# Block-diagonal column transforms of a Fourier mixing stage, issued as tiles of 64 rows

## The reference, cut to what matters

```python
xn = _layernorm(x, norm1_w, norm1_b)
xf = jnp.fft.rfft2(xn, axes=(1, 2), norm='ortho')          # (8, 32, 17, 192), complex
xf = xf.reshape(B, h, w // 2 + 1, NB, BS)                   # 8 channel blocks of 24
o1 = jnp.einsum('bhwni,hwnio->bhwno', xf, w1c) + b1c        # its own 24x24 matrix per (h, w, block)
o1 = jax.lax.complex(jax.nn.relu(o1.real), jax.nn.relu(o1.imag))
xs = jnp.fft.irfft2(o1.reshape(B, h, w // 2 + 1, C), s=(h, w), axes=(1, 2), norm='ortho')
xm = _layernorm(xs, norm2_w, norm2_b)
hdn = jax.nn.gelu(xm @ mlp_w1 + mlp_b1, approximate=False)
return xs + x + hdn @ mlp_w2 + mlp_b2
```

## Time and profile before

| | us |
|---|---|
| median of 3 runs (1192.73 to 1200.53) | 1198.21 |
| the profiled execution, its own time | 1196.19 |
| its span, first to last instruction | 1194.4 |
| mean granted clock of TensorE, as a share of full speed | 0.956 |
| TensorE busy / weight loads busy | 1079.7 / 875.7 |
| VectorE busy / ScalarE busy / GpSimd busy | 853.9 / 696.7 / 363.5 |

### The profile page before, as it was taken

One profiled execution on the slowest core, in us unless ns is written; L12 is line 12 of the kernel. 1 busy time (PEld: TensorE's weight loads), 2 busy tenths in 40 slices (PEclk: granted clock), 3 DMA queues, 4 the chain that ended last, 5 costly groups with the idle time before them and its releaser, 6 DMA issues. The chain is left out here.

```text
span 1194.4 us, 26159 instructions
## 1 busy us (share of the span) xinstructions
PE 1079.7 (90%) x9256; PEld 875.7 (73%) x9256; DVE 853.9 (71%) x2230; ACT 696.7 (58%) x1293; POOL 363.5 (30%) x383
## 2 busy tenths in 40 slices
PE   3659999985797999999799999999999699999998
PEld 1358888873486888888567767767677488888887
DVE  6645556442899988777768689689698767676665
ACT  3736556542664567666677567567545266766665
POOL 1250111211699200000238438338247311021110
PEclk9879999896898999999899999999999799999999
DMA  7888799896100000000100000000000000000001
GB/s 179 272 183 169 149 168 185 154 208 163 49 1 1 0 0 0 0 0 0 47 1 2 1 1 1 1 1 1 1 1 1 0 14 27 26 27 26 26 26 40
DMA packets 140186, 64.19 MB, mean 54 GB/s; under 512 B 115808, under 2 KB 134912, under 8 KB 140096
## 3 DMA queue, kind: packets, MB, share of 16 engines
q1 hardware_dynamic: 132888, 37.42, 15.5%
q0 software_dynamic: 5568, 18.73, 5.8%
q10 hardware_dynamic: 1648, 6.91, 1.8%
HBM read 44.17 MB, written 12.58 MB: 48 GB/s over the span
## 5 line engine op out<-in xcount | busy, mean ns | idle before, releaser
L904 ACT ACTIVATE L_conv_hf<-L_conv_ps,L_conv_b 128x512 f32<-128x512 f32 x192 | 132.1, 688 | 184.4 <-PE L_conv_ps L1075 175.7
L1094 PE MATMUL L_conv_ps<-w2hl,L_conv_hhi 128*128 128x384 f32 x768 | 229.2, 366 | 4.1 <-DVE X L990 4.1
L980 DVE TENSOR_TENSOR L_conv_hlo<-L_conv_hf,L_conv_hhi 128x512 fp32r<-128x512 f32 x192 | 140.9, 750 | 78.5 <-ACT L_conv_hhi L913 76.4
L1094 PE MATMUL L_conv_ps<-w2hl,L_conv_hlo 128*128 128x192 f32 x768 | 188.6, 252 | 0.0
L1209 POOL TENSOR_TENSOR sc_lo<-XS,sc_hi 128x512 fp32r<-128x512 f32 x96 | 142.9, 1504 | 116.1 <-ACT sc_hi L1285 116.1
L1487 PE MATMUL sc_ps<-sc_hi,wh 128*128 128x512 f32 (+1 forms) x440 | 160.8, 437 | 3.4 <-ACT XS L1269 3.2
L1094 PEld LDWEIGHTS L_conv_ps<-w2hl,L_conv_hhi 128*128 128x128 f32 x768 | 144.4, 188 | 8.7 <-DVE L_conv_hlo L980 3.4
L1487 PE MATMUL sc_ps<-sc_hi,wl 128*128 128x512 f32 (+1 forms) x440 | 147.8, 392 | 0.0
L1094 PEld LDWEIGHTS L_conv_ps<-w2hl,L_conv_hlo 128*128 128x128 f32 x768 | 146.2, 191 | 0.0
L636 PE MATMUL psF<-spectrum,X 100*24 100x64 f32 x4352 | 128.9, 290 | 15.2 <-issue 11.2
L861 POOL TENSOR_TENSOR X<-X,L_conv_b 128x192 f32 x128 | 83.2, 681 | 194.4 <-DVE L_conv_xn L964 194.4
(11 more groups left out here) (135 smaller groups left out, 2028.0 us busy)
## 6 DMA issues: line engine op xcount, KB each, us to landing
X<-in_L_conv_w SPq DMA_DIRECT2D x136, 144.0 KB
XS<-in_x POOLq DMA_DIRECT2D x8, 768.0 KB, 6.9
rows_spectrum<-XS POOLq DMA_DIRECT2D x8, 768.0 KB, 4.2
d<-rows_spectrum ACTq DMA_DIRECT2D x8, 768.0 KB, 5.5
X<-in_x SPq DMA_DIRECT2D x8, 768.0 KB, 8.2
out<-X SPq DMA_DIRECT2D x15, 384.0 KB, 2.6
XS<-d POOLq DMA_DIRECT2D x59, 96.0 KB, 4.7
spectrum<-in_L_conv_mlp_w SPq DMA_DIRECT2D x2, 576.0 KB, 9.3
```

Of the source, the lines that this page charges most:

```text
L904: nc.scalar.activation(hf[:, m % 3, :], ps[:, RB + m % 2, :], gelu, bias=b1[:, m:m + 1]).then_inc(act1, 1)
L980: nc.vector.tensor_tensor(hlo[:, m, :], hf[:, m % 3, :], hhi[:, m, :].bitcast(F32), ALU.subtract).then_inc(h_lo, 1)
L1094: mm = pe.matmul(o, x, w, start=(m == 0 and n == 0), stop=(m == MT - 1 and n == 1), skip_group_check=True)
```

## The change

The zero blocks of the two tables go. The forward table now holds `fc` twice, on partitions 0 to 63 and 64 to 127, 64 columns wide. `columns` issues for each batch two matmuls, one for each bin, with 64 rows of `d2` as weights and 64 columns of the table. Bin 0 goes to the first PSUM bank, bin 1 to the second, with all eight batches. The spread follows: VectorE now takes bin 0 of all batches, ScalarE bin 1, as 8 runs of 32 instead of 4 runs of 64. In unit 2 the two halves of the channels take the places of the bins, so that its spread has 12 operations on each engine instead of 24.

In `inverse`, for groups 1 to 7, each half is four matmuls of 64 rows by 64 columns instead of two of 128 by 128: row tile k is the bin, which writes bank 6 + k, and column tile j is the part of the batches. The copies out of PSUM double in number: each engine copies two pieces of 64 partitions by 384 instead of one of 128 by 384. A half now waits until all four copies of the half before it are done; before, each matmul waited for the copy of its own bank. Group 0, which mixes bins 0 and 16, keeps matmuls of 128 rows. Orders of rows in the tables change to suit, with no cost at run time. The loads of the constant tables get a little smaller.

Of `spread` and `inverse_out` the diff shows VectorE's; ScalarE's are alike, with `S[..., H:]` and bank `col_bank(u) + 1`, and with the upper partitions and bank 7. `lower` and `upper` are partitions 0 to 63 and 64 to 127. `copies(g, half)` is the number of copies that each engine has made once that half is out; `half_of(u, k)` is the half of the channels whose factor an engine's spread applies.

```diff
     def columns(u):
-                at = col_bank(u)
-                for b in range(B):
-                    bank, col = at + b // 4, P * (b % 4)
+                for b, k in itertools.product(range(B), range(2)):
+                    out = ps[0:HALF, col_bank(u) + k, 2 * H * b:2 * H * (b + 1)]
                     if units[u] is None:
-                        for s in range(2):
-                            out = ps[0:HALF, bank, col:col + P].rearrange("p (r f) -> p r f", r=2)[:, :, H * s:H * (s + 1)]
-                            mm = pe.matmul(out, d2[0][:, b, HALF * s:HALF * (s + 1)], fwd_h0[:, P:], start=True, stop=True)
+                        mm = pe.matmul(out, d2[0][:, b, HALF * k:HALF * (k + 1)], fwd_h0[:, 2 * H:], start=True, stop=True)
                     else:
-                        s = units[u][1]
-                        mm = pe.matmul(ps[0:HALF, bank, col:col + P], d2[g % 2][:, b, HALF * s:HALF * (s + 1)],
-                                       fwd_h0[:, 0:P] if g == 0 else fwd_h[:, :], start=True, stop=True)
-                mm.then_inc(hdft, 1)
+                        table, s, rows = fwd_h0 if g == 0 else fwd_h, units[u][1], (lower, upper)[k]
+                        mm = pe.matmul(out, d2[g % 2][rows, b, HALF * s:HALF * (s + 1)], table[rows, 0:2 * H],
+                                       start=True, stop=True)
+                    if b == B - 1:
+                        mm.then_inc(hdft, 1)
...
     def spread(u):
-                v = ps[0:HALF, col_bank(u), :].rearrange("p (b r f) -> p r b f", b=B // 2, r=2)
-                for cut, of in slots(u):
-                    for part, n in itertools.product(range(3), range(NH)):
-                        scale = (ngm if part == 0 else gm)[:, of, n:n + 1]
-                        nc.vector.tensor_scalar(S[u % 2][0:HALF, part, n, 0:B // 2, cut], v[:, int(part != 1), :, cut], scale,
-                                                None, ALU.mult).then_inc(spread_v, 1)
+                v = ps[0:HALF, col_bank(u), :].rearrange("p (b r h) -> p r b h", b=B, r=2)
+                for part, n in itertools.product(range(3), range(NH)):
+                    scale = (ngm if part == 0 else gm)[:, half_of(u, 0), n:n + 1]
+                    nc.vector.tensor_scalar(S[u % 2][0:HALF, part, n, :, 0:H], v[:, int(part != 1)], scale,
+                                            None, ALU.mult).then_inc(spread_v, 1)
...
     def inverse_out(g, half):
-                j = 2 * half
-                dve.wait_ge(inv_done, 4 * g + j + 1)
+                dve.wait_ge(inv_done, 8 * g + 4 * (half + 1))
...
-                nc.vector.tensor_copy(d3[g % 2][:, 384 * j:384 * j + 384], ps[:, 6, 0:384]).then_inc(d3_v, 1)
+                for to, fr, j in [(slice(0, P), slice(0, P), 0)] if g == 0 else [(lower, lower, 0), (lower, upper, 1)]:
+                    at = NH * HALF * (2 * half + j)
+                    nc.vector.tensor_copy(d3[g % 2][to, at:at + NH * HALF], ps[fr, 6, 0:NH * HALF]).then_inc(d3_v, 1)
...
     def inverse(g, half):
+                if g or half:
+                    before = copies(g, half - 1) if half else copies(g - 1, 1)
+                    pe.wait_ge(d3_v, before)
+                    pe.wait_ge(d3_a, before)
+                if g:
+                    for j, k in itertools.product(range(2), range(2)):
+                        rows, cols = (lower, upper)[k], (lower, upper)[j]
+                        at = 4 * NH * (2 * half + j)
+                        pe.matmul(ps[cols, 6 + k, 0:NH * HALF], inv_h[rows, 0:2 * H], z[rows, at:at + 4 * NH],
+                                  start=True, stop=True, skip_group_check=True).then_inc(inv_done, 1)
+                    return
                 for j in (2 * half, 2 * half + 1):
-                    if g or j >= 2:
-                        done = 4 * g + j - 2
-                        pe.wait_ge(d3_v if j % 2 == 0 else d3_a, done // 2 + 1)
...
```

More of the change, by code:

```diff
@@ L55, in order @@
         return np.arange(P).reshape(shape).transpose(axes).reshape(-1)
-    fwd_w = np.kron(eye, fw)[:, order((HH, NG, 4), (1, 0, 2))]
-    inv_w = np.kron(eye, iw)[order((HH, NG, 4), (0, 2, 1))]
-    spread = order((4, TPB, HH), (2, 0, 1))
-    parts = order((2, 2, H), (1, 0, 2))
-    halves = order((2, 2, 2, H // 2), (0, 2, 1, 3))
+    fwd_w = np.kron(eye, fw)[:, order((HH, NG, 2, 2), (1, 2, 0, 3))]
+    inv_w = np.kron(eye, iw)[order((HH, NG, 2, 2), (2, 0, 3, 1))]
+    spread = np.arange(2 * H).reshape(2, TPB, HH).transpose(2, 0, 1).reshape(-1)
+    halves = np.arange(2 * H).reshape(2, 2, H // 2).transpose(1, 0, 2).reshape(-1)
     fc = np.block([[co, -si], [si, co]])
@@ L69, in dft_tables @@
     z = np.zeros((2 * H, 2 * H))
[L70 to L84 removed]
+    real = fc.copy()
+    real[H:] = 0
+    nyquist = np.zeros((2 * H, 2 * H))
+    nyquist[H:] = fc[0:H]
+    fwd_h = np.concatenate([fc[spread], fc[spread]])
+    fwd_h0 = np.concatenate([np.concatenate([real[spread], fc[spread]]), np.concatenate([nyquist[spread], z])], 1)
+    ib = ic[halves][:, spread]
+    real, last = ic.copy(), np.zeros((2 * H, 2 * H))
+    real[:, H:] = 0
+    last[:, H:] = ic[:, 0:H]
+    real, last = real[halves][:, spread], last[halves][:, spread]
+    first = np.block([[real, z], [z, ib]])
+    inv_h = np.concatenate([np.concatenate([ib, ib]), first, np.block([[last, z], [z, z]]), np.block([[z, z], [last, z]])], 1)
+    return [np.ascontiguousarray(a.astype(np.float32)) for a in (fwd_w, inv_w, fwd_h, fwd_h0, inv_h)]
 def block_ones():
@@ L303, in operations, with half_of, copies @@
         def operations(u, engine):
-            halves = 2 if units[u] is None else 1
-            return 3 * NH * halves + (NH if u < 2 and engine == "v" else 0)
+            return 3 * NH + (NH if u < 2 and engine == "v" else 0)
         spread_by = {e: list(itertools.accumulate(operations(u, e) for u in range(UNITS))) for e in "va"}
-        def slots(u):
-            if units[u] is None:
-                return [(slice(H * s, H * (s + 1)), s) for s in range(2)]
-            return [(slice(0, 2 * H), units[u][1])]
+        lower, upper = slice(0, 2 * H), slice(2 * H, P)
+        def half_of(u, k):
+            return k if units[u] is None else units[u][1]
+        def copies(g, half):
+            n = 2 * g + half + 1
+            return n if g == 0 else 2 * n - 2
         def col_bank(u):
@@ L362, in _ @@
                 sp.dma_start(dst, src).then_inc(sh.raw_in, 16)
-            sp.wait_ge(d3_v, 2 * NG)
-            sp.wait_ge(d3_a, 2 * NG)
+            sp.wait_ge(d3_v, copies(NG - 1, 1))
+            sp.wait_ge(d3_a, copies(NG - 1, 1))
             for k in (0, 3, 6):
@@ L458, in inverse_out @@
             def inverse_out(g, half):
-                j = 2 * half + 1
-                act.wait_ge(inv_done, 4 * g + j + 1)
+                act.wait_ge(inv_done, 8 * g + 4 * (half + 1))
                 if g >= 2 and half == 0:
                     act.wait_ge(sh.rows_in[g % 2], 16 * TPB * (g // 2))
-                nc.scalar.activation(d3[g % 2][:, 384 * j:384 * j + 384], ps[:, 7, 0:384], ACT.Copy).then_inc(d3_a, 1)
+                for to, fr, j in [(slice(0, P), slice(0, P), 1)] if g == 0 else [(upper, lower, 0), (upper, upper, 1)]:
+                    at = NH * HALF * (2 * half + j)
+                    nc.scalar.activation(d3[g % 2][to, at:at + NH * HALF], ps[fr, 7, 0:NH * HALF],
+                                         ACT.Copy).then_inc(d3_a, 1)
             spread(0)
@@ L480, in _ @@
                 inverse_out(NG - 1, half)
-            act.wait_ge(d3_v, 2 * NG)
-            act.wait_ge(d3_a, 2 * NG)
+            act.wait_ge(d3_v, copies(NG - 1, 1))
+            act.wait_ge(d3_a, copies(NG - 1, 1))
             for k in (2, 5):
```

59 lines of the change are left out of this document (22 added, 37 removed).

## The result

| | before | changed |
|---|---|---|
| median of 4 runs each, same chip | 1195.47 (1190.28 to 1200.53) | 1205.58 (1197.64 to 1211.55) |
| ratio, with its 95% interval | | 1.0074 [1.0038, 1.0111] |
| the profiled execution, its own time | 1196.19 | 1197.64 |
| its span | 1194.4 | 1195.7 |
| mean granted clock of TensorE | 0.956 | 0.944 |

The forecast was 1190.0, within 1181 to 1203. The profiled execution of the changed kernel is the fastest of its four, so its trace shows too little of the loss.

A forecast was written before the change was run, and what follows sets the result against it. TensorE's own order was taken as the path in the changed stage. Terms -5.0 - 0.7 - 5.4 + 2.0 + 0.8 + 1.5 = -6.8 us gave 1189.4 from 1196.2, or 1191.4 from the median; forecast 1190, range 1181 to 1203.

The forecast's parts named there:

- Tiles overlap: Column transforms and inverses: matmuls on different tiles run at once; column transform 1.82 to 1.46 us, inverse half 1.30 to 0.81.
- two deep: Rival, 15%: tiles overlap only two deep, an inverse half takes 5 streams instead of 2.5; total 1200 us.
- no overlap: Rival, 6%: fp32 matmuls in these tiles don't overlap at all; +36 us, total 1232.
- 0.026 us a record: Products in four column tiles: the record rate that does not change with the clock, taken as the issue rate.
- bound of 14 us of loss for the columns: Column transforms of units 3 to 16: the loss if row tiles don't overlap, 32 x 0.086 = 2.75 us each.
- Change of shape, the term of +2.0 us: Column transform and inverse now differ in tile shape: 0.2 us lost in each of 10 cycles, units 5 to 14.
- -5.0, -5.4 and +2.0: Gains of 14 column transforms (0.36 us each) and 11 inverse halves (0.49 each), and the loss by tile-shape changes.
- Units 0 and 1: First column transforms, at half clock: the first unit goes from some 3.4 to 2.7 us, gain 0.7.
- Instructions, the term of +1.5 us: 148 matmuls a cycle instead of 138: gaps grow with fetches per us, about 13%, from 11.2 to 12.7 us.
- fetches and DMA take the gain back: Rival, 22%: faster cycles want instructions and weights sooner, the 11.2 us of gaps grow by half; total 1194 us.
- The sign that I had named: Forecast called wrong if the granted clock of this stretch falls below the 0.94 of before.
- The end: Transpose to last scatter: second half waits for four copies, two on each engine; 3.71 to 4.5 us, loss 0.8.

The follow-up runs named there:

- light_defer: Kernels before and changed, without mix-weight loads after the first four units and with four x loads moved to the next stage: 0.9916 and 0.9856 of the kernel before.
- after_shift: Changed kernel with 40 small matmuls ahead of the first one, shifting the borders of its instruction blocks: 1.0046 of the kernel before.
- tail_after: Changed kernel with the first half of the last group's inverse writing banks 4 and 5, free by then: 1.008 of the kernel before.
- shifted kernels: Kernel before with 24 and changed kernel with 40 small matmuls ahead of the first, shifting instruction-block borders: 1.0026 and 1.0046 of the kernel before.

## Why the prediction was wrong, point by point

**Tiles overlap: right.** At full clock a half of the inverse is 0.80 us (forecast 0.81; before it was 1.39, where the sum took 4 x 0.325 = 1.30) and a column transform 1.50 (forecast 1.46, before 1.82). The rivals "two deep" (1.7) and "no overlap" (2.7) fall. The first of them leaned on the Trainium skill, page "TensorE: Matmul & The Clock Gate", section Part 3, where matmuls start and end in strict order. The changed kernel's trace has the starts of a half: the first records of the four tiles at 222.80 to 222.82 us, all within 0.02 us, the second ones at 223.17 to 223.19. They start in an order, then, but no tile waits for the second record of another. (The prediction's 0.026 us a record of the products is a little low, as its windows count records that reach in from outside; start to start it is 7.33 / 256 = 0.029, about 0.028 without the change of shape, and nothing in the sum hangs on the difference. Its bound of 14 us of loss for the columns is 13 by its own terms.)

**Change of shape, the term of +2.0 us: nothing of it shows.** A change between 128 and 64 rows costs 0.1 us, not 0.2, in the kernels with one part alone; between the forward and the inverse tiles of the changed kernel there is no such step. All together, at full clock: columns -4.3 and inverses -6.3 in the stage, where -5.0, -5.4 and +2.0 were written, so 2.2 us better than forecast.

**Units 0 and 1: right**, -0.7 us.

**Instructions, the term of +1.5 us: the step that failed.** It measured +6.7 us (12.8 to 19.5). I scaled all stops with the number of fetches per us. The runs show that traffic makes the fetches late: without the later mix weights most of the mid stops go, without the loads of x those of the end. Ten more matmuls in a longer cycle didn't add any. A faster cycle under the same traffic fits both, but is argued, not shown. The stops at the end, 4.9 of the 11.2 us in the earlier trace rows, have another source, the loads of x, and I hadn't asked what lay beside that 4.89. My rival "fetches and DMA take the gain back" named the mechanism, but its "grow by half" was applied to a sum that had no other loss.

**No term for the clock: the second failure.** I took the clock of before as given. The sign that I had named came: over 170.5 to 257.4 us the granted clock is 0.86 and 0.83 in the two traces of the changed kernel, against 0.94 and 0.98. In the two traces of each kernel TensorE spent 34 and 30 us of this stage at half clock before, 57 and 81 in the changed kernel. The products don't feel it (0.028 us a record at either clock), but what the change touched does: above what they take at full clock, columns and inverses lost 5.0 and 2.9 us before, 4.9 and 13.4 after. That is +5.2 on average, and what turns -10.6 into -5.4. What precedes a fall is mostly a stop of the products, as at 238.44. But the stops are only one half of it: with tiles a stretch at half clock also lasts longer. From 95 us to the end of the stage the two traces of before have 11 such stretches, eight of 3.4 us and three of 6.8; those of the changed kernel have 18, seven of 3.4, eight of 6.8, one of 10.2 and two, at the end, of 24 and 34 that reach into the next stage. In the `light_defer` pair, with hardly a stop, half clock took 15 us of this stage before and 31 with the tiles, and there one stop of 1.9 us, up to 249.73, is followed by 24 us of it. With the forward tiles alone all four stretches behind 95 us are of 6.8 us; with the inverse tiles alone most are of 3.4, and the last is of 34. What in the tiles holds the clock down isn't shown.

**The end: mis-sized.** +2.4 us instead of +0.8. Over half of it is the clock again: both traces of the changed kernel are at half clock there. In `after_shift`, where it is whole for the first of the two last halves, the end is 10.3 us and not 11.0, 0.7 us for that half; twice that is 1.4 (an estimate, as no trace has both at full clock), which leaves 1.0. I also hadn't counted that VectorE's copy of group 6 behind the transpose became two: from the end of the transpose to the next matmul it is 1.27 us instead of 0.58. `tail_after` takes that wait away.

**What stays open.** The balance of the stage gives +3.2 us (+3.5 with the shifted kernels' traces added), the medians 9 to 10. Up to 2 us more lie behind the stage: from its first matmul to the first of the scan the first MLP takes 270.6 to 271.1 us in seven of the nine traces with inverse tiles, 268.3 to 268.8 in all of the others. I know no reason; it wasn't tried. The spans of the four traces of both kernels differ by 8.1 us on average, of which 3.6 lie ahead of the first column transform; but its start scatters from 69.7 to 77.4 us over all traces, with means of 74.2 without tiles and 74.0 with them, so I can't charge that to the change. The rest of the medians' loss, some 4 us, has no place that I can show: each profile is of one execution, and stops and clock differ from run to run. Nor is it shown why a fetch starts late under load: the queue, or the memory behind it.

## What to carry to other kernels

Where TensorE stops at a fixed distance in instructions and the DMA engines are nearly full, price the stops first: here a change that makes the work between two fetches shorter met more of them, and then had its own instructions at half clock. Moving transfers that nobody waits for yet out of that stretch gained 0.6% with four lines, where the tiles lost 0.7 to 0.9%. And when a copy becomes two, look what stands ahead of them at the end, where nothing covers them.

## What the runs showed of the hardware

- Four tiles of 64 by 64 take fp32 matmuls of 384 columns at 0.80 us for 8 records, against 1.39 for 4 records of the full array: 42% less for the same work.
- Two row tiles with 64 columns go at 1.50 / 32 = 0.047 us a record, at half clock at 2.75 / 32 = 0.086. The forecast's 0.086 a pair was 0.043 a record.
- The products, in four column tiles of 24, keep 0.028 us a record at either clock, while the wider matmuls around them take nearly twice as long at half clock: 2.75 us instead of 1.50 for a column transform, 1.49 instead of 0.80 for a half of the inverse.
- Instructions come as blocks of 16 KB through a DMA queue of their own on the same 16 engines. With these at 0.84 busy TensorE stood for 11 to 18 us of the stage; with the share at 0.40 the stops of its regular cycles fell from 8.3 to 0.9 us, and from 11.2 to 2.7.
- The tiles lower the granted clock beyond what their stops explain: 0.962 without and 0.951 with them, where the stops of the stage are down to 1.6 and 3.7 us. Why is open.
- Of the four tiles' records the first four start within 0.02 us, the second four 0.37 us later: the second record of one tile holds up no other tile.
